# One block for the remainders of gate and value columns in two middle layers, and no swapped base columns in the last layer

## The reference, cut to what matters

```python
HID = int(DIM * 4 * 2 / 3)                 # 682
...
h = shift_token(x)
h = layernorm(h) * lg + lb
h = h @ w1 + b1                            # 256 -> 2 * 682
a, g = jnp.split(h, 2, axis=-1)
h = a * jax.nn.gelu(g, approximate=False)
x = x + h @ w2 + b2                        # 682 -> 256
...
E, S = 512, 128
uv = jax.nn.silu(xn @ uv_w.T + uv_b)       # 256 -> 2 * E + S
u, v, base = (uv[..., :E], uv[..., E:2 * E], uv[..., 2 * E:])
base = base[:, :, None, :] * gamma[None, None] + beta
base = _rope(base)                         # needs base and base with its two halves swapped
q, k = (base[:, :, 0, :], base[:, :, 1, :])
kernel = jnp.square(jax.nn.relu(q @ k.T / SQRT_S + bias[None]))
out = u * (kernel @ v)
return out @ o_w.T + o_b + shortcut
```

## Time and profile before

| what | value |
|---|---|
| median of 3 runs | 2621.67 us (2618.68 to 2624.2) |
| the profiled execution's own time | 2619.7 us |
| its span, first to last instruction | 2617.9 us |
| mean granted TensorE clock | 0.969 of full speed |
| PE busy | 95% of the span |
| DVE, ACT, POOL busy | 76%, 62%, 42% |
| stage a | 0 to about 562 us |
| stage b (32 steps) | about 565 to 1879 us |
| stage c | about 1882 us to the end |

### The profile page before, as it was taken

One profiled execution on the slowest core, in us unless ns is written; L12 is line 12 of the kernel. 1 busy time (PEld: TensorE's weight loads), 2 busy tenths in 40 slices (PEclk: granted clock), 3 DMA queues, 4 the chain that ended last, 5 costly groups with the idle time before them and its releaser, 6 DMA issues. The chain is left out here.

```text
span 2617.9 us, 57926 instructions
## 1 busy us (share of the span) xinstructions
PE 2478.5 (95%) x20386; PEld 2245.2 (86%) x20386; DVE 1992.0 (76%) x5970; ACT 1616.4 (62%) x3738; POOL 1111.2 (42%) x969
## 2 busy tenths in 40 slices
PE   7999999978999999999999999999669999899997
PEld 6999999977899999988889999999658887788886
DVE  6899999857888888888888888887366556755554
ACT  4788888836877877877878778778245113431111
POOL 3232333225455455455454554453145334533332
PEclk7999999989999999999999999999789999999999
DMA  2011221122222222233322222222332012221111
GB/s 79 24 36 36 93 68 50 33 77 73 85 87 80 89 87 82 88 99 100 108 84 90 86 82 88 87 80 90 102 111 84 34 33 85 89 73 33 33 33 41
DMA packets 223622, 190.39 MB, mean 73 GB/s; under 512 B 22373, under 2 KB 205801, under 8 KB 222313
## 3 DMA queue, kind: packets, MB, share of 16 engines
q1 hardware_dynamic: 204616, 177.04, 21.3%
q10 hardware_dynamic: 18720, 9.64, 1.3%
...
## 5 line engine op out<-in xcount | busy, mean ns | idle before, releaser
L2153 ACT ACTIVATE c_kern_hi<-c_kern 128x512 fp32r<-128x512 f32 x128 | 81.1, 634 | 365.4 <-DVE c_kern L2275 365.4
L1372 ACT ACTIVATE b_sb_probs<-b_sb_probs,b_sb_neg_top,b_sb_r_norm 128x256 f32<-128x256 f32 x512 | 301.7, 595 | 3.1 <-DVE b_sb_neg_top L1510 2.3
L2056 POOL TENSOR_TENSOR c_kern_lo<-c_kern,c_kern_hi 128x512 fp32r<-128x512 f32 x128 | 171.9, 1344 | 292.0 <-ACT c_kern_hi L2153 292.0
L1277 POOL TENSOR_TENSOR b_sb_r_norm<-b_sb_squares,b_sb_power 128x8 f32<-128x8 f32 x64 | 105.1, 1642 | 353.8 <-DVE b_sb_squares L1460 353.8
L39 PE MATMUL psum<-b_sb_fT_lo,b_sb_w_hi 128*128 128x256 f32 x768 | 224.4, 292 | 13.2 <-DVE b_sb_mid L1572 6.5
L41 PE MATMUL psum<-b_sb_fT_hi,b_sb_w_hi 128*128 128x256 f32 x768 | 217.1, 283 | 0.0
L40 PE MATMUL psum<-b_sb_fT_hi,b_sb_w_lo 128*128 128x256 f32 x768 | 216.9, 282 | 0.0
L1503 DVE CUSTOM_DVE_ANT_0 b_sb_probs<-psum,b_sb_mask 128x256 f32<-128x256 f32 x512 | 195.3, 419 | 11.9 <-DVE b_sb_mid L1572 10.6
L39 PE MATMUL psum<-c_kern_lo,c_v_hi 128*128 128x512 f32 x512 | 204.3, 399 | 0.0
L41 PE MATMUL psum<-c_kern_hi,c_v_hi 128*128 128x512 f32 x512 | 200.5, 392 | 0.0
L40 PE MATMUL psum<-c_kern_hi,c_v_lo 128*128 128x512 f32 x512 | 200.4, 392 | 0.0
...
## 6 DMA issues: line engine op xcount, KB each, us to landing
...
Y<-b_sb_y SPq DMA_DIRECT2D x128, 128.0 KB, 2.1
...
b_sb_x_f<-Y SPq DMA_DIRECT2D x128, 64.0 KB, 1.9
...
```

Source lines behind the costliest of these rows:

```text
L1277: pool.tensor_tensor(r, s, p, ALU.pow).then_inc(r_ready[1][b], 1)
L1372: ins = act.activation(probs[b][:, n, :], probs[b][:, n, :], ACT.Exp, bias=neg_top[b][:, n:n + 1], scale=r_norm[b][:, h:h + 1], accum_out= ...
L2056: pool.tensor_tensor(kern_lo[i % RING][:], kern[i % RING][:], kern_hi[i % RING][:].bitcast(F32), ALU.subtract)\
```

## The change

Middle layers: the last block's 42 gate columns and 42 value columns share one block of 128 columns, gates in rows 0 to 63 (`LOW`), values in rows 64 to 127 (`HIGH`). So there are 11 column blocks of `w1`, not 12, and `up` with m = 5 has 6 matmuls, not 12. ACT reads the low rows and writes `gate` in the high rows; DVE reads value and gate in the high rows and writes `mid` in the low rows; the high part goes to the low rows of `mid_hi`, the low part to its high rows. `w2_both` holds the last block of `w2` twice, in both halves, and `down` has 2 matmuls for the last block, not 3. `w2_both` is written by two more ACT instructions in the setup and two at the switch of layers.

Last stage: the swapped base columns are gone. `base` on PE is 6 matmuls; ACT writes the swapped copy with two instructions of 64 rows each, from the other half of the rows. There are 10 one-column bias products, not 12. DVE reads the `shifts` results in a function of its own behind `turn_h(0)`. SP's slot runs `next_rope` and `u` first, then `residual`, then `load`.

```diff
-                for n in (2 * m, 2 * m + 1):
+                for n in range(2 * m, min(2 * m + 2, n_in)):
                     out = ring.out(t, ("w", m), 512)[:, n % 2 * 256:n % 2 * 256 + 256]
...
                 for m in range(B_FC):
                     if b == 0:
                         pe.wait_ge(mid_lo_ready, t * B_FC + m + 1)
-                    ins = product3(pe, ring.out(t, ("y", b), D), mid_hi[:, m, tok], mid_lo[:, m, tok], w2_hi[:, m, :],
-                                   w2_lo[:, m, :], m == 0, m == B_FC - 1)
+                    out = ring.out(t, ("y", b), D)
+                    if m < rest:
+                        product3(pe, out, mid_hi[:, m, tok], mid_lo[:, m, tok], w2_hi[:, m, :], w2_lo[:, m, :], m == 0, False)
+                    else:
+                        pe.matmul(out, mid_hi[:, m, tok], w2_lo[:, m, :], start=False, stop=False)
+                        ins = pe.matmul(out, mid_hi[:, m, tok], w2_both[:], start=False, stop=True)
...
+                for to in (LOW, HIGH):
+                    act.activation(w2_both[to, :], w2_raw0[LOW, rest, :], ACT.Copy)
...
-                act.activation(gate[m % 2][:], ring.out(t, ("w", m), 512)[:, 0:256], ACT.Gelu, bias=b1[:, t // NT, 2 * m:2 * m + 1])\
-                   .then_inc(gate_ready, 1)
+                to, of = (slice(0, P), slice(0, P)) if m < rest else (HIGH, LOW)
+                act.activation(gate[m % 2][to, :], ring.out(t, ("w", m), 512)[of, 0:256], ACT.Gelu,
+                               bias=b1[of, t // NT, 2 * m:2 * m + 1]).then_inc(gate_ready, 1)
...
-                ring.read(t, dve.scalar_tensor_tensor(out=mid[m % 2][:], in0=ring.out(t, ("w", m), 512)[:, 256:512],
-                                                  scalar=b1[:, t // NT, 2 * m + 1:2 * m + 2], in1=gate[m % 2][:],
+                to, of, n = (slice(0, P), slice(0, P), 2 * m + 1) if m < rest else (LOW, HIGH, 2 * m)
+                ring.read(t, dve.scalar_tensor_tensor(out=mid[m % 2][to, :], in0=ring.out(t, ("w", m), 512)[of, n % 2 * 256:n % 2 * 256 + 256],
+                                                  scalar=b1[of, t // NT, n:n + 1], in1=gate[m % 2][of, :],
...
+                    ins = dve.tensor_tensor(mid_hi[HIGH, m, :], mid[m % 2][LOW, :], mid_hi[LOW, m, :].bitcast(F32), ALU.subtract)
...
             for slot in range(first_slot, last_slot):
+                for n in step_in(slot):
+                    next_rope(n)
+                    u(n)
+                for n in step_in(slot + 1):
+                    residual(n)
                 for n in step_in(slot + 4):
                     load(n)
-                for n in step_in(slot + 1):
-                    residual(n)
-                for n in step_in(slot):
-                    u(n)
-                    next_rope(n)
...
-                for k in range(2):
-                    ins = act.activation(base[:, k, :], ring.out(("base", n), 512)[:, k * C_STEP:(k + 1) * C_STEP], ACT.Silu,
-                                         bias=b_col[:, C_EC + k:C_EC + k + 1])
+                act.activation(base[:, 0, :], ring.out(("base", n), C_STEP), ACT.Silu, bias=b_col[:, C_EC:C_EC + 1])
+                for to, of in ((slice(0, HALF), slice(HALF, C_S)), (slice(HALF, C_S), slice(0, HALF))):
+                    ins = act.activation(base[to, 1, :], ring.out(("base", n), C_STEP)[of, :], ACT.Silu, bias=b_col[of, C_EC:C_EC + 1])
...
-                for k in range(2):
-                    ins = columns(n, ("base", n), k, 2 * C_E + k * P)
-                ring.written(ins, ("base", n))
+                ring.written(columns(n, ("base", n), 0, 2 * C_E), ("base", n))
...
                     turn_h(n)
+                    if n == 0:
+                        shifts()
```

More of the change, by code:

```diff
@@ L34 @@
 B_FC = -(-B_HID // P)
+B_IN = 2 * B_FC - 1
+B_REST = B_HID - (B_FC - 1) * P
+LOW, HIGH = slice(0, P // 2), slice(P // 2, P)
 def product3(pe, out, w_hi, w_lo, x_hi, x_lo, first, last):
@@ L969, in layer_b @@
     pairs = B_HEADS // 2
-    n_in = 2 * B_FC
+    n_in, rest = B_IN, B_FC - 1
     def head_at(n):
@@ L1001, in layer_b @@
         w2_lo_at, w2_lo = here(), sb("w2_lo", [P, B_FC, D], F32R)
+        w2_both = sb("w2_both", [P, D], F32R)
         b1 = sb("b1", [P, B_LAYERS, n_in])
@@ L1163, in next_part, with in_cols @@
             return ((wo_next[:], wo_hi[:], wo_lo[:]), (w2_next[:], w2_hi[:], w2_lo[:]))[n - 3]
+        def in_cols(m):
+            return slice(2 * m * P, min(2 * m + 2, n_in) * P)
         @block.sync
@@ L1424, in mid_ @@
                 act.wait_ge(mid_ready, t * B_FC + m + 1)
-                act.activation(mid_hi[:, m, :], mid[m % 2][:], ACT.Copy).then_inc(mid_hi_ready, 1)
+                at = slice(0, P) if m < rest else LOW
+                act.activation(mid_hi[at, m, :], mid[m % 2][at, :], ACT.Copy).then_inc(mid_hi_ready, 1)
             def swap(t, n):
@@ L1430, in swap @@
                     act.wait_ge(next_in[n], 16)
+                    if n == 4:
+                        for to in (LOW, HIGH):
+                            act.activation(w2_both[to, :], w2_next[LOW, rest, :], ACT.Copy)
                     act.activation(hi, raw, ACT.Copy).then_inc(next_hi, 1)
@@ L1580, in mid_ @@
                 dve.wait_ge(mid_hi_ready, t * B_FC + m + 1)
-                dve.tensor_tensor(mid_lo[:, m, :], mid[m % 2][:], mid_hi[:, m, :].bitcast(F32), ALU.subtract)\
-                   .then_inc(mid_lo_ready, 1)
+                if m < rest:
+                    ins = dve.tensor_tensor(mid_lo[:, m, :], mid[m % 2][:], mid_hi[:, m, :].bitcast(F32), ALU.subtract)
+                else:
+                    ins = dve.tensor_tensor(mid_hi[HIGH, m, :], mid[m % 2][LOW, :], mid_hi[LOW, m, :].bitcast(F32), ALU.subtract)
+                ins.then_inc(mid_lo_ready, 1)
             def down(t, b):
@@ L1777 @@
 C_W = 2 * P - 1
-C_PROJ = 2 * C_E + 2 * C_S
+C_PROJ = 2 * C_E + C_S
+HALF = C_S // 2
 C_STEP = 2 * P
@@ L1783 @@
 C_TILES = BATCH * C_CHUNKS * NT
-C_EARLY = {"ident": (P,), "w_raw": (KC, C_PROJ), "b_v_raw": (C_E,), "d_w": (KC, D), "rows": (2 * D,), "x_in": (2, D), "y_in": (2, D), "gb": (2, KC)}
+C_EARLY = {"ident": (P,), "w_raw": (KC, C_PROJ), "b_v_raw": (C_E,), "d_w": (KC, D), "rows": (2 * D + KC * C_S,), "x_in": (2, D), "y_in": (2, D), "gb": (2, KC)}
 C_LINE = 2 * SEQ
@@ L1906, in layer_c @@
         ones, total, delta = over("ones", kern_at, [P, P]), over("total", kern_at + 512, [P, 1]), over("delta", kern_at + 544, [P, 2])
-        b_raw = over("b_raw", kern_at + 608, [P, C_EC + 2])
+        b_raw = over("b_raw", kern_at + 608, [P, C_EC + 1])
         ring = Slots(sem, psum, "c_ring", list(bank_uses()))
@@ L2218, in weights @@
                 ring.wait_full(dve, ("shifts", 1))
-                ring.read(dve.tensor_tensor(b_col[:], ring.out(("shifts", 0), C_EC + 2), b_raw[:], ALU.add), ("shifts", 0))
+                ring.read(dve.tensor_tensor(b_col[:], ring.out(("shifts", 0), C_EC + 1), b_raw[:], ALU.add), ("shifts", 0))
                 ring.read(dve.tensor_tensor(b_v_raw[:], ring.out(("shifts", 1), C_E), b_v_raw[:], ALU.add), ("shifts", 1))
@@ L2364, in shifts @@
                 ring.wait_bank(pe, ("shifts", 0))
-                for n, col in enumerate(list(range(0, C_E, P)) + [2 * C_E, 2 * C_E + P]):
+                for n, col in enumerate(list(range(0, C_E, P)) + [2 * C_E]):
                     for c in range(KC):
-                        ins = pe.matmul(ring.out(("shifts", 0), C_EC + 2)[:, n:n + 1], w_raw[:, c, col:col + P], gb[:, 1, c:c + 1],
+                        ins = pe.matmul(ring.out(("shifts", 0), C_EC + 1)[:, n:n + 1], w_raw[:, c, col:col + P], gb[:, 1, c:c + 1],
                                         start=(c == 0), stop=(c == KC - 1))
@@ L2582, in gates_and_values @@
 def gates_and_values(w):
-    pad = np.zeros(w.shape[:-1] + (B_FC * P - B_HID,), w.dtype)
-    a, g = (np.concatenate([part, pad], -1).reshape(w.shape[:-1] + (B_FC, P)) for part in (w[..., :B_HID], w[..., B_HID:]))
-    return np.stack([g, a], -2).reshape(w.shape[:-1] + (2 * B_FC * P,))
+    a, g = w[..., :B_HID], w[..., B_HID:]
+    whole = B_HID - B_REST
+    pairs_ = np.stack([part[..., :whole].reshape(w.shape[:-1] + (B_FC - 1, P)) for part in (g, a)], -2)
+    pad = np.zeros(w.shape[:-1] + (P // 2 - B_REST,), w.dtype)
+    return np.concatenate([pairs_.reshape(w.shape[:-1] + (2 * whole,)), g[..., whole:], pad, a[..., whole:], pad], -1)
 def layout(i):
@@ L2606, in layout @@
         "b2_gb": np.stack([cols(f["ln_g"]), cols(f["ln_b"])], 2),
-        "c_w": rows(np.concatenate([uv_w, swapped(uv_w[:, 2 * C_E:])], 1)),
-        "c_b_col": cols(np.concatenate([uv_b[:C_E], uv_b[2 * C_E:], swapped(uv_b[2 * C_E:])])),
+        "c_w": rows(uv_w),
+        "c_b_col": cols(np.concatenate([uv_b[:C_E], uv_b[2 * C_E:]])),
         "c_b_v": uv_b[C_E:2 * C_E],
```

15 lines of the change are left out of this document (9 added, 6 removed).

## The result

| | median | runs | profiled execution, span |
|---|---|---|---|
| before | 2620.66 us | 4, 2618.68 to 2624.2 | 2619.7, 2617.9 us |
| after | 2600.38 us | 4, 2598.57 to 2606.37 | 2600.23, 2598.4 us |

The ratio is 0.9925, with a 95% interval of 0.9906 to 0.9945: 20 us faster. The direction was forecast, the size was not (46 us, range down to 24).

The account below looks back on a forecast made before the run. PE was taken to bound the middle layers, a latency chain the last stage's start. Savings of 27.5 + 0.5 + 11.5 + 6.2 = 45.7 us from 2619.7 gave 2574.0, with 2.0 added for the median 2576; range 2564 to 2597.

Parts of the forecast that it names:

- What bounds the kernel: Middle layers: PE is the bound, 449.93 us of work in 455; last stage's start: a chain of latencies.
- Part 1: Middle layers, PE: 8 matmuls fewer per step over 32 steps save 27.5 us, between 15 and 30.5.
- the middle layers return half: Rival: order tables fitted to old lengths and handed-on waits leave 15 us for 27.5, 2588 us; chance 0.14.
- does not do what it says: Rival: removed matmuls stood beside a chain everywhere; only setups and start gain, 12 us, 2610 us; chance 0.02.
- Part 2: Middle layers, ACT and DVE: instructions on 64 rows cost the same as full ones, so nothing.
- The chain to `down`: Middle layers: Gelu, multiply, high, low of block 5 end before `down` needs them, 1.5 us in hand.
- Part 3: Setups: fewer bias products save 0.5 us, between 0 and 0.9.
- Part 4: Start of last stage: earlier Silu and first rotation, no table wait for the second; 11.5 us, between 5 and 14.
- Part 5: Last stage, other 14 slots with projections: 6 matmuls fewer each, partly lost to longer waits; 6.2 us, between 4 and 9.9.
- all lower ones: Whole kernel: lower ends of all terms, 15 + 0 + 5 + 4 = 24 us, giving 2598 us.
- Wrong would be: steps above 38.4 us: Sign in the profile after: middle-layer steps were expected at 38.0 us; above 38.4 would show the forecast wrong.
- The other one: Sign in the profile after: PE's idle share in the middle layers' steps under 2.5%.

Follow-up runs that it names:

- e14: Kernel before, with DVE's low parts of mid(3) and mid(4) made one instruction instead of two: 2601.82 us against 2618.52 for before.
- e1: Kernel before with only the middle-layer part of the change: 2617.72 us against 2620.39 for before.
- e4: Kernel before with 8 matmuls per step fewer on PE, ACT and DVE instructions all on full rows: 2618.63 us against 2620.39 for before.
- e11: Kernel before with only the change's SP order in the last stage: 2611.12 us against 2618.89 for before.
- e2: Kernel before with only the last-stage part of the change: 2609.08 us against 2620.39 for before.

## Why the prediction was right and wrong

**What bounds the kernel; Part 1 (27.5 us, measured 2.8): wrong.** The step that failed is "DVE has 455 - 388.94 = 66 us idle in 11.7 steps, 5.6 us a step, ACT more, so 0.95 us less per step leaves both below the limit". Idle time summed over an engine is no slack when it lies in a loop with another engine. DVE (20.7 us, from 910.78 to 931.43, in its second half tied to POOL) and ACT (to the gate at 949.24) make up the 39.1 us one after the other. PE, at 98.9% busy, stood 0.65 us a step below it (39.09 - 38.44, with the step of e14 taken as PE's own) already before the change. The rival "the middle layers return half" had the cause in part ("ACT and DVE hand waits on"), but it spoke of the order tables as a matter of a few waits; "does not do what it says" came nearest for this stage, and had 0.02. The evidence against both, 449.93 of 455, was true and beside the point: two limits within 1.7% of each other look the same in busy time.

**Part 2 (0, measured about 0.1 us a plain step): small, as forecast, but for another reason.** The 64-row instructions last what full ones do (0.49 us for `mid`, 0.42 for its low part, against 0.47 and 0.41 in before). What they cost is the overlap with their neighbours. Before:

```profile
931.44 0.68 DVE L1566 TENSOR_TENSOR b_sb_fT_lo<-psum,b_sb_fT_hi 128x512 fp32r<-128x512 f32 x1
932.04 0.41 DVE L1581 TENSOR_TENSOR b_sb_mid_lo<-b_sb_mid,b_sb_mid_hi 128x256 fp32r<-128x256 f32 x1
932.37 0.42 DVE L1503 CUSTOM_DVE_ANT_0 b_sb_probs<-psum,b_sb_mask 128x256 f32<-128x256 f32 x1
```

After:

```profile
929.45 0.68 DVE L1581 TENSOR_TENSOR b_sb_fT_lo<-psum,b_sb_fT_hi 128x512 fp32r<-128x512 f32 x1
930.17 0.42 DVE L1600 TENSOR_TENSOR b_sb_mid_hi<-b_sb_mid,b_sb_mid_hi 64x256 fp32r<-64x256 f32 x1
930.62 0.42 DVE L1518 CUSTOM_DVE_ANT_0 b_sb_probs<-psum,b_sb_mask 128x256 f32<-128x256 f32 x1
```

Distances of 0.60 and 0.33 became 0.72 and 0.45, and that from `hT_lo` to `mid` went from 0.33 to 0.45: three times 0.12 us, the forecast's "0.09 us" a place from the rule of the Trainium skill ("VectorE: DVE Perf Modes", section "Two Vector instructions with no wait between them"). With the rule, the rows agree. Only I had put them into "DVE's 5.6 idle", and they stand in the loop: e1, with them, has a plain step of 39.18, e4, without, 39.04, and the kernels with the middle layers of before 39.05 to 39.09. Most of the 0.36 is given back where `neg_top` is held less by POOL, 0.33 us for 0.57; 0.12 is left. The chain to `down` got no wait, as forecast.

**Part 3 (0.5)** is too small to be seen in the total, but its row can be read: the bias products take 9.52 us for 10.37, 0.85 less as forecast, and PE's next matmul starts 0.2 us sooner after their start (11.16 us for 11.38). So about 0.2 us of it arrived.

**Part 4 (11.5, measured 12.3): right.** The start of the stage in after, with its first normalisation at 1882.77 (1887.00 in before); the offset of 4.23 us is taken off below:

```profile
1893.69 1.28 ACT L2138 ACT_TABLE_LOAD   x1 [7.67 <-PE psum L44]
```

```profile
1898.80 1.29 DVE L2276 TENSOR_TENSOR c_turned<-c_turned,c_rope 128x512 f32<-128x512 f32 x2 [0.46 <-ACT c_turned L2147]
1908.47 1.29 DVE L2276 TENSOR_TENSOR c_turned<-c_turned,c_rope 128x512 f32<-128x512 f32 x2
1911.80 0.69 DVE L2287 TENSOR_TENSOR c_qk_lo<-c_turned,c_qk_hi 128x512 fp32r<-128x512 f32 x1
```

Silu's table load is 7.4 us sooner than in the earlier trace rows (6.4 forecast), the first rotation 6.6 (6.0), the second has no wait for its table, and the second `c_qk_lo` is 12.3 sooner (11.6). ACT's wait of 6.53 us for the store of `U` is gone, too. SP's order alone moved the second rotation by 5.7 us in e11, as the term said (5.6).

**Part 5 (6.2, lower bound 4, measured 3.3): mis-sized.** From the second rotation to the sixteenth the lead over before grows only from 12.3 to 15.0 us, and to the end to 15.6. The waits for the line that drains the bank grew by more than the 0.37 us each (0.71 less on PE's way, 0.34 of it gained) that the term charged: in after

```profile
PE psum L42 <- DVE c_kern L2297: 19.8, 4, 5.6
PE psum L2414 <- DVE c_kern L2297: 13.6, 7, 4.3
```

against 18.1 and 9.4 in the earlier trace rows: 5.9 us more over 11 waits, 0.54 each, so 0.17 of the 0.71 was left where 0.34 had been counted (e2 has the same 19.8 and 13.6).

**The number.** Measured 2.8 + 12.3 + 3.3 = 18.4 against 45.7; the rest of the 20.3 us between the medians is within what executions differ by. The range ended at 2597 because it took "all lower ones" to hold 15 us from the middle layers. No row had excluded 0 there, and a lower end of 0 would have given 2613. The tell-tale I had named did its work: "Wrong would be: steps above 38.4 us". The other one did not: PE's idle share in the plain steps came out at 2.5%, as the forecast had it, though PE has some 37.5 us of work (38.44 - 8 x 0.119) in 39.18.
